# First batch of a fused attention and linear kernel: order of the first stacks, of the second batch's projections and of a load

## The reference, cut to what matters

```
x = x + proj(softmax(q k^T / 4) v)   with q, k, v = layernorm(x) @ qkv_w^T + qkv_b, 16 heads of 16
x = x + linear(fp8(layernorm(x)))    with a 256 x 256 weight, scales and a bias
```

## Time and profile before

| | |
|---|---|
| time, median of 3 runs | 931.93 us (931.64 to 932.08) |
| time of the profiled execution | 932.24 us |
| its span, first to last instruction | 930.4 us |
| TensorE matmul busy | 912.7 us, 98% |
| VectorE busy | 836.2 us, 90% |
| ScalarE busy | 667.5 us, 72% |
| GpSimd busy | 514.4 us, 55% |
| mean granted TensorE clock | 1.000 |

### The profile page before, as it was taken

One profiled execution on the slowest core, in us unless ns is written; L12 is line 12 of the kernel. 1 busy time (PEld: TensorE's weight loads), 2 busy tenths in 40 slices (PEclk: granted clock), 3 DMA queues, 4 the chain that ended last, 5 costly groups with the idle time before them and its releaser, 6 DMA issues.

```text
span 930.4 us, 17052 instructions
## 1 busy us (share of the span) xinstructions
PE 912.7 (98%) x5901; PEld 434.3 (47%) x5901; DVE 836.2 (90%) x1264; ACT 667.5 (72%) x1294; POOL 514.4 (55%) x528
## 2 busy tenths in 40 slices
PE   7999999999999999999999999999999999998997
PEld 5444444445444454544445444444544445443336
DVE  6978899898999989899998989999898998899986
ACT  3277767777776777777777777777777677776784
POOL 4533449285573937638294664829556492833433
PEclk9999999999999999999999999999999999999999
DMA  7864607556281644718355380745538064470101
GB/s 199 139 104 85 100 25 132 74 76 111 52 142 38 120 66 79 127 37 144 52 104 81 66 143 24 143 66 91 93 59 142 10 127 59 66 118 3 47 1 47
DMA packets 46206, 78.92 MB, mean 85 GB/s; under 512 B 10088, under 2 KB 13288, under 8 KB 46120
## 3 DMA queue, kind: packets, MB, share of 16 engines
q1 hardware_dynamic: 45352, 76.65, 46.7%
q10 hardware_dynamic: 768, 1.18, 0.8%
HBM read 17.90 MB, written 8.39 MB: 28 GB/s over the span
## 4 chain that ended last, share of the span: by engine, by line
PE 93%; DVE 3%; ACT 2%; DMA 1%; issue 1%; SPq 0%; POOL 0%; ACTq 0%; DVEq 0%; POOLq 0%
PE ps_t L609 28%; PE ps_o L649 27%; PE ps_m L464 10%; PE ps_s L628 8%; PE ps_m L515 6%; PE ps_m L550 5%; PE ps_m L584 3%; ACT pt L797 2%; PE ps_s L534 1%; PE ps_m L527 1%; DVE mx L1013 1%; PE ps_m L567 1%; PE ps_s L486 1%; DMA qs<-nmax 1%; DMA xin<-in_x 0%
## 5 line engine op out<-in xcount | busy, mean ns | idle before, releaser
L797 ACT ACTIVATE pt<-ps_t 128x512 f32<-128x512 f32 x1008 | 548.8, 599 | 187.5 <-PE ps_t L609 183.6
L1013 DVE TENSOR_REDUCE mx<-ps_s 128x2 f32<-128x1024 f32 x512 | 611.5, 1207 | 43.0 <-PE ps_s L628 40.9
L609 PE MATMUL ps_t<-qs,ks 50*128 50x512 f32 x1008 | 375.5, 449 | 7.0 <-ACT pt L797 6.8
L628 PE MATMUL ps_s<-ks,qs 48*128 48x512 f32 x1024 | 375.1, 450 | 0.0
L609 PEld LDWEIGHTS ps_t<-qs,ks 50*128 50x128 f32 x1008 | 159.8, 184 | 286.4 <-ACT pt L797 206.0
L649 PE MATMUL ps_o<-pt,vt 128*32 128x512 f32 x2048 | 272.4, 604 | 0.0
L1341 POOL TENSOR_TENSOR on<-ot,rden 128x256 f32<-128x256 f32 x63 | 39.1, 621 | 225.5 <-DVE rden L1074 225.5
L628 PEld LDWEIGHTS ps_s<-ks,qs 48*128 48x128 f32 x1024 | 158.4, 184 | 6.6 <-DVE mx L1013 4.0
L464 PE MATMUL ps_m<-xnT_p,wqkv_p 128*128 128x512 f32 x360 | 109.1, 420 | 0.1
L1332 POOL TENSOR_TENSOR parts<-parts 128x512 f32<-128x512 f32 x60 | 81.6, 1360 | 4.9
L649 PEld LDWEIGHTS ps_o<-pt,vt 128*32 128x32 f32 x2048 | 40.5, 108 | 88.2 <-issue 81.8
(11 more groups left out here) (145 smaller groups left out, 836.3 us busy)
## 6 DMA issues: line engine op xcount, KB each, us to landing
qs<-parts SPq DMA_DIRECT2D x186, 128.0 KB, 4.4
ks<-parts SPq DMA_DIRECT2D x180, 128.0 KB, 5.2
xin<-in_x SPq DMA_DIRECT2D x16, 512.0 KB, 3.6
xres<-in_x SPq DMA_DIRECT2D x15, 512.0 KB, 5.7
out<-h SPq DMA_DIRECT2D x29, 256.0 KB, 2.6
qs<-nmax SPq DMA_DIRECT2D x256, 4.0 KB
pt<-in_qkv_wT SPq DMA_DIRECT2D x1, 768.0 KB, 5.2
qs<-parts SPq DMA_DIRECT2D x12, 64.0 KB, 3.4
```

What stands on the lines that cost most here:

```text
L609: nc.tensor.matmul(t_bank(b, s, g), ks[par][rows, slot, keys], qs[par][rows, slot, :], start=True, stop=True).then_inc(st_done, 1)
L628: done = nc.tensor.matmul(ps_s[:, s % 2, g, :], qs[par][rows, slot, queries], ks[par][rows, slot, :], start=True, stop=True)
L797: nc.scalar.activation(pt[n % 2][:, w % 2 + 2 * a, w // 2, :], t_bank(b, s, a), ACT.Exp, scale=SCALE).then_inc(exp_done, 1)
L1013: dve.tensor_reduce(mx[:, r, :, s % QUARTER], ps_s[:, s % 2, :, :], AX_X, ALU.max).then_inc(max_done, 1)
```

## The change

Every edit is in slots 0 and 1.

1. **First stack.** SyncE issues q of the first half (six DMAs), then four of the six of k of the first half (high part for r = 2, low part for r = 1); ScalarE issues the other two. SyncE then issues q and k of the second half, as before in 12 DMAs.
2. **TensorE at the end of slot 0** no longer waits for the last low part and for v; the five unread matmuls go to `ps_o`. The transposes of batch 1's x move to steps 1 and 2 of slot 1, and with them ScalarE's two copies and its six DMAs of k of heads 8 to 15.
3. **Projections of batch 1** go to steps 5 to 16, three steps each with two matmuls, n = 1 and 3 in bank `ps_o`. Their products come in another order, so that the first three need only one half of the transposed x.
4. **Values and transposes** of slot 1 go from steps 20, 22, 24, 26 to 22, 24, 26, 28.
5. **Layer norm of batch 2:** VectorE's sums go from the end of slot 0 to steps 15 to 18 of slot 1, its end to step 19; GpSimd's part goes behind the last split of batch 1.
6. **SyncE in slot 1** issues the first maxima's rows ahead of the load of batch 3's x.
7. **Unread matmuls** in steps 0 to 15: 11 instead of 22, four of them in step 15.

The diff, cut to its core:

```diff
-PROJECT_QK_1 = (range(4, 10), range(10, 16), (16, 17), (18, 19))
+PROJECT_QK_1 = ((5, 6, 7), (8, 9, 10), (11, 12, 13), (14, 15, 16))
+TRANSPOSE_X_1 = (1, 2)
+VALUES_AND_X_1 = (22, 24, 26, 28)
...
+LN1_SUM_1 = (15, 16, 17, 18)
+LN1_END_1 = 19
...
-WARM_STEPS = (2, 2, 2, 2, 1, 1, 1, 1, 3, 1, 1, 1, 1, 1, 1, 1)
+WARM_STEPS = (2, 0, 0, 2, 2, 0, 0, 0, 1, 0, 0, 0, 0, 0, 0, 4)
...
+        def qk_bank(b, n):
+            if b == 0:
+                return ps_s[:, n // 2, n % 2, :]
+            return ps_o[:] if b == 1 and n % 2 else ps_m[:]
...
-                for half in range(2):
-                    sp.wait_ge(whole_ready, 1)
-                    for r in (0, 1):
-                        copy_first(sp, qs, 0, Q_PARTS, r, half)
-                    sp.wait_ge(low_ready, 1)
-                    copy_first(sp, qs, 0, Q_PARTS, 2, half)
+                sp.wait_ge(whole_ready, 1)
+                for r in (0, 1):
+                    copy_first(sp, qs, 0, Q_PARTS, r, 0)
+                sp.wait_ge(low_ready, 1)
+                copy_first(sp, qs, 0, Q_PARTS, 2, 0)
                 sp.wait_ge(low_ready, 2)
+                copy_first(sp, ks, 1, K_PARTS, 1, 0)
+                copy_first(sp, ks, 1, K_PARTS, 2, 0)
+                for r in (0, 1, 2):
+                    copy_first(sp, qs, 0, Q_PARTS, r, 1)
                 for r in (0, 2, 1):
                     copy_first(sp, ks, 1, K_PARTS, r, 1)
                 stack(0, 0, 2)
...
+                if u == 1:
+                    rows(0, 0, 0)
                 if present(-2):
                     load(u + 2, par)
-                if u == 1:
-                    rows(0, 0, 0)
...
                 if part == 0:
-                    take_bank("project_qk", n, u)
-                    if n == 0:
+                    if u > 1 or n % 2 == 0:
+                        take_bank("project_qk", n, u)
+                    if u > 1 and n == 0:
                         pe.wait_ge(xnT_low, 2 * u + 2)
+                    if u == 1 and n == 1:
+                        pe.wait_ge(xnT_ready, 6)
+                    if u == 1 and n == 3:
+                        pe.wait_ge(whole_ready, 4 + 2)
...
-                pe.wait_ge(low_ready, 4)
-                pe.wait_ge(v_ready, 4)
                 for i in range(WARM_SCORES):
-                    nc.tensor.matmul(ps_s[:, 1, 1, :], wqkv_p[:, 0, 0, 0:P], wqkv_p[:, 0, 0, 0:S], start=True, stop=True)
-                for c in range(NC):
-                    transpose_x(1, c)
+                    nc.tensor.matmul(ps_o[:], wqkv_p[:, 0, 0, 0:P], wqkv_p[:, 0, 0, 0:S], start=True, stop=True)
...
-            def stack_k(half):
+            def stack_k():
                 act.wait_ge(whole_ready, 2)
-                for r in (0, 2):
-                    copy_first(act, ks, 1, K_PARTS, r, half)
-                act.wait_ge(low_ready, 2)
-                copy_first(act, ks, 1, K_PARTS, 1, half)
+                copy_first(act, ks, 1, K_PARTS, 0, 0)
...
+                    if u == 1 and s in TRANSPOSE_X_1:
+                        copy_xnT(1, TRANSPOSE_X_1.index(s))
+                    if u == 1 and s == TRANSPOSE_X_1[1]:
+                        stack_second_k()
...
                 finish_bias()
-                for j in range(NJ):
-                    ln1_sum(2, 0, j)
-                ln1_finish(2)
```

More of the change, by code:

```diff
@@ L453, in project_qk @@
             def project_qk(u, n, part, parts):
-                bank = ps_m[:]
+                bank = qk_bank(u, n)
                 if part == 0:
-                    take_bank("project_qk", n, u)
-                    if n == 0:
+                    if u > 1 or n % 2 == 0:
+                        take_bank("project_qk", n, u)
+                    if u > 1 and n == 0:
                         pe.wait_ge(xnT_low, 2 * u + 2)
+                    if u == 1 and n == 1:
+                        pe.wait_ge(xnT_ready, 6)
+                    if u == 1 and n == 3:
+                        pe.wait_ge(whole_ready, 4 + 2)
                 first = (n % 2) * D + (n // 2) * P
                 products = [(pw, px, c) for pw, px in PAIRS for c in range(NC)]
+                if u == 1:
+                    products = [(pw, px, c) for c in range(NC) for pw, px in PAIRS]
                 for m in range(6 * part // parts, 6 * (part + 1) // parts):
                     pw, px, c = products[m]
+                    if u == 1 and n == 0 and m % 3 == 0:
+                        pe.wait_ge(xnT_low, 2 + c + 1)
                     last = nc.tensor.matmul(bank, wqkv_p[:, pw, c, first:first + P], xnT_p[:, px, c, :],
@@ L638, in values @@
                         pe.wait_ge(v_ready, NJ * b + NJ)
+                    if n == 0 and b == 0:
+                        pe.wait_ge(whole_ready, 4 + 4)
                     early = 2 if b == B - 1 and n == UNITS - 1 else 0
@@ L684, in slot @@
                         linear(u - 3, LINEAR.index(s))
-                    if s in VALUES_AND_X and present(0):
-                        values_and_x(u, VALUES_AND_X.index(s))
+                    steps_vx = VALUES_AND_X_1 if u == 1 else VALUES_AND_X
+                    if s in steps_vx and present(0):
+                        values_and_x(u, steps_vx.index(s))
                     if s in PROJECT_OUT[0] and present(2, B - 1):
@@ L704, in bias, with unread @@
                 last.then_inc(bias_done, 1)
-            def unread(count):
+            def unread(count, bank=ps_t[:, 1, :]):
                 for i in range(count):
-                    nc.tensor.matmul(ps_t[:, 1, :], wqkv_p[:, 0, 0, 0:P], wqkv_p[:, 0, 0, 0:S], start=True, stop=True)
+                    nc.tensor.matmul(bank, wqkv_p[:, 0, 0, 0:P], wqkv_p[:, 0, 0, 0:S], start=True, stop=True)
             def project_last(bank, t, half, picks):
@@ L839, in copy_qk @@
                 t, bias = n // 2, bias_column(b, n)
-                bank = ps_s[:, n // 2, n % 2, :] if isinstance(b, int) and b == 0 else ps_m[:]
+                bank = qk_bank(b, n)
                 act.wait_ge(qk_done, 4 * b + n + 1)
@@ L861, in copy_hqT, with stack_second_k @@
                                bank.bitcast(BF16).rearrange("p (c n) -> p c n", c=NC)[:, :, tok]).then_inc(hqT_ready, 1)
-            def stack_k(half):
+            def stack_k():
                 act.wait_ge(whole_ready, 2)
-                for r in (0, 2):
-                    copy_first(act, ks, 1, K_PARTS, r, half)
-                act.wait_ge(low_ready, 2)
-                copy_first(act, ks, 1, K_PARTS, 1, half)
+                copy_first(act, ks, 1, K_PARTS, 0, 0)
+            def stack_second_k():
+                act.wait_ge(low_ready, 4)
+                for r, part in enumerate(K_PARTS):
+                    for g in range(2):
+                        rows = slice(HALF * g + HD * r, HALF * g + HD * (r + 1))
+                        act.dma_start(ks[0][rows, NS:2 * NS, :].bitcast(F32),
+                                      parts[HALF * g:HALF * (g + 1), 3, part, :]).then_inc(stacked[1][0], 16)
             def first_slot():
@@ L877, in first_slot @@
                 copy_qk(0, 0, 1)
-                stack_k(0)
+                stack_k()
                 copy_qk(0, 0, 2)
@@ L882, in first_slot @@
                 copy_first_v(1)
[L883 to L890, removed]
             def slot(u, par, present):
@@ L1154, in slot @@
                         finish_linear(u - 3, LINEAR.index(s))
[L1156 to L1159, removed]
+                    if present(-1) and u > 0:
+                        steps_sum, step_end = (LN1_SUM_1, LN1_END_1) if u == 1 else (LN1_SUM, LN1_END)
+                        if s in steps_sum:
+                            ln1_sum(u + 1, 1 - par, steps_sum.index(s))
+                        if s == step_end:
                             ln1_finish(u + 1)
@@ L1400, in slot @@
                     split_lin()
-                    layernorm_x(2, 0)
                 if present(2):
@@ L1417, in slot @@
                     split(u, 3)
-                if present(-1) and u != 1:
+                if present(-1):
                     layernorm_x(u + 1, 1 - par)
```

13 lines of the change are left out of this document (9 added, 4 removed).

## The result

The changed kernel takes **942.68 us** (median of four executions, 941.19 to 943.92) against 931.96 for the kernel before: 1.0102 times as long, 95% interval 1.0065 to 1.0139. Forecast was 931.2. Run again beside other kernels it took 942.87 (941.02 to 944.58 in four executions; 1.0101, 1.0062 to 1.0139). The loss is there in every execution.

The account below looks back on a forecast made before the run. TensorE, with 93% of the chain, was taken as the bound. Gains of 0.85 us at step 16 and 0.1 for its transposed maxima, less 0.27 in steps 28 to 30, made 931.93 - 0.7 = 931.2 us; range 930.1 to 932.6.

Parts of the forecast that it names:

- Start of step 0: Slot 1: the first stack lands earlier, so step 0 starts at 22.1 in place of 23.55, 1.45 us gained.
- rival A: Step 0: the first stack lands no earlier, as engines share the 16 DMA engines; 932.2 us, chance 0.16.
- Steps 0 to 15: Slot 1: maxima's pace stays, step 8's wait counted at nothing (1.1 at worst), 0.2 saved; step 15 starts at 39.5.
- Rival D: Steps 3 to 15: TensorE's clock drops to 1.2 GHz, 0.6 us lost in each of 13, 8 us; chance 0.02.
- The landing at step 16: Copies of heads 8 to 15, then rows, land; step 16 starts at 41.7 in place of 42.55, 0.85 us gained.
- rival B: Ahead of step 16: everything behind the first stack is issued 2.3 to 2.5 later; step 16 at 43.6, 933.1 us; chance 0.15.
- Steps 16 to 31: Slot 1: VectorE's layer norm leaves nothing of the removed projections; step 23 at 54.65 against 54.62; 0.27 lost in steps 28 to 30.
- The wait of TensorE for GpSimd's normalization in step 22: Slot 1: TensorE is there at 53.7, its transposes need the normalization, ready at 54.2; a sign of the forecast.
- The loss in steps 28 to 30: Slot 1: a fourth piece of value projections and transposes makes a pair 3.44 in place of 3.17, 0.27 us lost.
- The later slots: From 130 us on TensorE is always busy; slot 2 starts about 0.7 us earlier and every later slot shifts the same.
- a shift that changes after slot 2: Sign of being wrong: the shift against the kernel before changes from slot to slot after slot 2.

Follow-up runs that it names:

- e4: The changed kernel with the old order of the first copies on SyncE and ScalarE (six each, then the second half): 940.59 us.
- e1: The changed kernel with ScalarE's six 128 KB copies of k issued only after the second half of the first stack has landed: 935.52 us.
- e7: The changed kernel with four of six second-half copies of k issued by ScalarE behind v, and two unread matmuls in each of steps 17 to 21: 934.20 us.
- e10: e7 with 14 in place of 4 unread matmuls in step 15: 932.58 us.
- e8: e7 with batch 1's projection n = 3 in steps 16 to 18 in place of unread matmuls there, unread ones in 14 and 19 to 21: 938.30 us.
- e12: e8's order of copies, but ScalarE's six large copies right behind the second half's; projections in steps 10 to 19, unread matmuls in steps without extras: 932.59 us.
- e13: e12 with GpSimd's normalization of batch 2 ahead of batch 1's last split, and the second maxima's rows ahead of batch 1's second stack: 930.15 us.
- e5: e4 with two unread matmuls in each of steps 17 to 21: 933.48 us (931.84 to 945.53).

## Why the prediction was wrong

**Start of step 0: right.** Forecast 22.1, measured 21.66; the landings took 2.2 to 2.8 us, as the first ones before. e4, with the old order back and all else changed, starts step 0 at 24.69, so the order is what won it. The rule that was set against it (rival A; the Trainium skill, "DMA: Bandwidth & Descriptors", section "Issuing engines are not separate DMA queues") has two halves. The second, that starting transfers from several engines only saves initiation time, doesn't cover what happened: with fewer copies beside them the landings took 2.2 to 2.8 us in place of 4.2 to 5.2. The first, that transfers from different engines interleave on the same 16 DMA engines, agrees with the trace and is what bit at step 8.

**Steps 0 to 15: the step that failed.** "Step 8 waits for the second half: its twelfth DMA is issued at 26.8 and lands at 29.5 to 32.0 [...] Taken at nothing, 1.1 at worst." It was issued at 27.6 and landed 7.2 us later, and step 8 waited 4.5 us. The upper end was the 5.2 us of the earlier trace rows, measured with two queues of 64 KB copies. In the new order the neighbours on the other queue are copies of 128 KB. The nearest rows at hand for that were the earlier trace rows, where copies of 128 KB among others of their size landed 9.6 us after their issue, and the landing of SyncE's issues 21.8 to 24.3 in the kernel before, just as ScalarE's large ones began at 23.74, 4.0 us at most:

```profile
DMA to landing us min/median/max: 2.6/2.8/4.0
```

The row with the wrong neighbours was used. By the 1.0 us for 128 KB of the earlier trace rows, and half of it for 64 KB, an estimate is that SyncE's last four copies and ScalarE's six, all issued from 24.97 on, need 8 us: 33, a good deal nearer to the 34.8. I had worked out that ScalarE's copies would start at 26.0, before SyncE's last ones, and asked only what that did to step 16. Step 15 shows that the rest of this sum held: forecast at 39.5, it starts at 39.4 in e1, 39.3 in e7 and 39.1 in e10.

**The clock: the second failed step, and the dear one.** Rival D had the size (8 us; measured 8.1 to 8.6) by luck: it put the fall in steps 3 to 15, 0.6 us in each, where the clock was low in steps 8 to 15 (a step took 1.87 us there, 39.02 to 40.89, against 1.1) and again from 58.8 to 69 us. It had a chance of 0.02, on the ground that "the new order keeps two extras in nearly every step". That looked at steps 0 to 15 and at work alone. It missed that a wait of 4.5 us is itself a stretch without work, and that steps 16 to 21 lose theirs: ten of twelve projection matmuls (four from the pair 16 and 17, six from 18 and 19; the text had "five or six" from each), and the value projections of step 20. That removal was booked there as a possible gain only.

**The landing at step 16: near, on the late side.** Forecast 41.7, ends 41.3 and 43.6. With step 8 mended it was 42.5 (e8), 43.3 (e7, e10; in e10 TensorE's own unread matmuls end then too) and 43.7 (e1), towards the end where the whole train shifts. Each of these runs moved the copies as well, so none shows the changed kernel's own landing without the wait. It is still evidence that rival B's mechanism was real, behind the larger loss.

**Steps 16 to 31: about right at full clock.** In e10 step 23 starts 11.6 us behind step 16, where 12.1 was forecast and 12.07 stood before: 0.4 gained, with VectorE nearly without idle time in steps 17 to 20, as forecast. The wait of TensorE for GpSimd's normalization in step 22 was 0.8 us in e12; in e10 a weight load alone waited 0.3. The loss in steps 28 to 30 came as forecast: steps 28 and 29 take 3.45 us in e10 (63.62 to 67.07) in place of 3.17.

**The later slots: not quite.** "A later slot cannot absorb or win anything by a shift at its start", and the last section named a shift that changes after slot 2 as a sign of being wrong. It does change: slot 2 starts 12.6 us later than before, slot 16 11.6. First the kernel before, then the changed one, each at slots 2 and 16:

```profile
69.46 0.29 PEld L628 LDWEIGHTS ps_s<-ks,qs 48*128 48x128 f32 x2
...
838.75 0.29 PEld L628 LDWEIGHTS ps_s<-ks,qs 48*128 48x128 f32 x2
...
82.09 0.29 PEld L646 LDWEIGHTS ps_s<-ks,qs 48*128 48x128 f32 x2
...
850.35 0.29 PEld L646 LDWEIGHTS ps_s<-ks,qs 48*128 48x128 f32 x2
```

Most of that 1.0 us goes in steps of some 0.06 per slot: 55.06 us for a slot in the one trace (not "some 49", as the section on the time before has it), 55.00 in the other. e13 shows it too: 1.4 us ahead at slot 2, 2.2 at slot 16. Not every run does (e4 is 4.0 late at both), and the cause stays open.

## What to carry to other kernels

When a set of transfers is moved to another queue or later on it, ask for every gate which transfers will run beside it in the new order, and take the landing time from rows with those neighbours. On a core whose TensorE is kept warm by unread matmuls, price each new wait twice: its own length, and what stands behind it at the lower clock (here 1.87 us for a step in place of 1.1); useful work moved out of a stretch has to be replaced there. When such a loss shows, fill the waits first: it tells in one run how much is clock and how much is order.

## What the runs showed that I had not expected

Idle times of some 2 us stood ahead of a fall in some executions: at step 16 in e7 and e8, and ahead of step 0 in e5, where the clock then stayed at 0.50 for 33 us although TensorE was busy for 32.92 of 33 by its records. Nor was an idle time needed: between step 16 and e4's fall none is above 0.4 us. And filling gaps made the times steadier, not only shorter: ten executions within 0.4 us in e12, where e4's ten span 12 us and the kernel before, in e12's round, 7 us.
